# Where the last four outputs of an attention stage stand in the program order of the stage behind it

## What is computed

```python
x = L0_attn_x
x = _layernorm(x + _L0_attn_ref(x, ...), axis=-1)      # stage A: chunked linear attention
x = _layernorm(x + _L0_ffn_ref(x, ...), axis=-1)       # stage B: fp8 feed-forward
x = _layernorm(x + _L1_attn_ref(x, ...), axis=-1)      # stage C: causal softmax attention, one head of 128
x = _layernorm(x + _L1_ffn_ref(x, ...), axis=-1)       # stage D: base matrix + shared and routed low-rank parts
```

## Time and profile before

| | us |
|---|---|
| median of 3 runs | 1538.15 (1537.54 to 1539.66) |
| the profiled execution's own time | 1542.17 |
| its span, first to last instruction | 1540.5 |
| PE busy | 1470.2 (95%) |
| DVE busy | 1007.8 (65%) |
| ACT busy | 734.6 (48%) |
| POOL busy | 342.3 (22%) |
| mean granted TensorE clock | 0.984 |

### The profile page before, as it was taken

One profiled execution on the slowest core, in us unless ns is written; L12 is line 12 of the kernel. 1 busy time (PEld: TensorE's weight loads), 2 busy tenths in 40 slices (PEclk: granted clock), 3 DMA queues, 4 the chain that ended last, 5 costly groups with the idle time before them and its releaser, 6 DMA issues.

```text
span 1540.5 us, 23863 instructions
## 1 busy us (share of the span) xinstructions
PE 1470.2 (95%) x9484; PEld 1008.8 (65%) x9484; DVE 1007.8 (65%) x1967; ACT 734.6 (48%) x1040; POOL 342.3 (22%) x259
## 2 busy tenths in 40 slices
PE   8999999999999978899999999999999999999998
PEld 6677777777777766444555554546666665667886
DVE  3355646464645354897787778774888888666665
ACT  4333333332333323688768867863433444432333
POOL 0021212121111122000000000000666776760001
PEclk9999999999999999999999999999999999999999
DMA  7203031213030250101001101002300000000112
GB/s 266 80 27 108 27 108 55 83 52 107 29 107 13 75 191 13 37 0 56 28 29 55 55 1 55 1 26 74 91 1 1 1 1 1 0 1 28 55 55 82
DMA packets 43904, 79.93 MB, mean 52 GB/s; under 512 B 7073, under 2 KB 14881, under 8 KB 42386
## 3 DMA queue, kind: packets, MB, share of 16 engines
q1 hardware_dynamic: 43794, 78.41, 14.9%
HBM read 53.24 MB, written 25.17 MB: 51 GB/s over the span
## 4 chain that ended last, share of the span: by engine, by line
PE 61%; issue 19%; DVE 14%; ACT 3%; POOL 2%; DMA 0%; SPq 0%; DVEq 0%; POOLq 0%; ACTq 0%
PE psum L125 12%; PE psum L127 12%; PE psum L126 12%; PE psum L1335 6%; PE psum L978 3%; PE psum L985 3%; DVE sm L447 3%; PE psum L594 2%; PE psum L1313 2%; PE psum L620 2%; PE psum L615 2%; PE psum L609 2%; DVE c_mx L1256 1%; PE psum L624 1%; PE psum L629 1%
## 5 line engine op out<-in xcount | busy, mean ns | idle before, releaser
L978 PE MATMUL psum<-early,high 128*128 128x512 fp8e4 x1024 | 234.9, 382 | 10.2 <-DVE low_r L950 4.1
L978 PEld LDWEIGHTS psum<-early,high 128*128 128x128 fp8e4 x1024 | 98.2, 98 | 132.4 <-ACT early L857 6.6
L1184 POOL TENSOR_TENSOR c_ls<-c_ls,c_pr 128x512 f32<-128x512 f32 (+2 forms) x136 | 161.8, 1190 | 63.9 <-ACT c_pr L1229 54.5
L393 POOL TENSOR_TENSOR rms<-ms,mhalf 128x16 f32<-128x16 f32 x32 | 93.1, 2910 | 365.6 <-DVE ms L456 365.6
L1229 ACT ACTIVATE c_pr<-c_sc 128x512 f32<-128x512 f32 (+2 forms) x144 | 85.1, 594 | 151.5 <-DVE c_sc L1271 136.5
L1335 PE MATMUL psum<-c_pr,V 128*128 128x512 f32 (+2 forms) x288 | 138.3, 566 | 3.7 <-ACT c_pr L1229 2.5
L125 PE MATMUL psum<-Qh_r,Kh 128*128 128x512 f32 (+1 forms) x272 | 140.0, 515 | 0.0
L1271 DVE TENSOR_TENSOR c_sc<-psum,c_mb 128x512 f32<-128x512 f32 (+2 forms) x144 | 91.8, 640 | 42.8 <-PE psum L127 32.8
L985 PE MATMUL psum<-high,b_act 128*128 128x512 fp8e4 x512 | 117.3, 383 | 2.4 <-DVE Ql_r L955 2.2
L125 PE MATMUL psum<-early_r,high_r 128*128 128x512 f32 x256 | 107.1, 418 | 5.5 <-DVE early_r L419 5.5
L126 PE MATMUL psum<-Ql_r,Kh 128*128 128x512 f32 (+1 forms) x272 | 104.9, 386 | 0.0
(11 more groups left out here) (230 smaller groups left out, 3250.7 us busy)
## 6 DMA issues: line engine op xcount, KB each, us to landing
low<-x_dram SPq DMA_DIRECT2D x9, 1024.0 KB, 5.6
wst<-in_L_ffn_w_gating SPq DMA_DIRECT2D x16, 512.0 KB, 4.6
xs<-in_L_attn_x SPq DMA_DIRECT2D x8, 1024.0 KB, 7.9
xt<-in_x_turned SPq DMA_DIRECT2D x7, 1024.0 KB, 4.8
x_dram<-xs SPq DMA_DIRECT2D x7, 1024.0 KB, 4.8
x_dram<-low SPq DMA_DIRECT2D x5, 1024.0 KB, 4.3
wst<-in_L_ffn_w_linear SPq DMA_DIRECT2D x16, 256.0 KB, 4.6
high<-x_dram SPq DMA_DIRECT2D x4, 1024.0 KB, 6.4
```

The source lines that it names most:

```text
L393: nc.gpsimd.tensor_tensor(rms[:, :], ms[:, :], const["mhalf"][:, 0:H], ALU.pow).then_inc(*done)
L978: last = t.matmul(out[:, h, :], w8g[:, tile + k, (2 * m + h) * P:(2 * m + h + 1) * P], x8[:, u, k, :], start=k == 0, stop=k == DC - 1)
L1184: nc.gpsimd.tensor_tensor(ls[:, i % 2, q0:], ls[:, i % 2, q0:], pr[:, g % SLOTS, q0:], ALU.add).then_inc(*L.done(*name))
```

## The change

The plan's two lines that placed the four outputs of block 7, in pairs around hN, rb and rr of chunk 1 of block 0, are replaced by a loop that puts one output behind each of (rr, 0, 1), (rr, 0, 3), (rr, 1, 1) and (rr, 1, 3). The PSUM banks of the four outputs become 0, 5, 0, 5 in place of 7, 0, 1, 2.

```diff
         elif kind == "y" and i == NB - 1:
-            w = (7, 0, 1, 2)[name[2]]
+            w = (0, 5, 0, 5)[name[2]]
         else:
             w, n_m = (3, 4, 7)[n_m % 3], n_m + 1
...
         plan += part("D", ("hT", 0), ("rb", 0, 0)) + [("C", ("L", last))] + part("D", ("rb", 0, 0), ("h", 1))
-        plan += part("C", ("L", last), ("y", last, 1)) + part("D", ("h", 1), ("rr", 0, 1)) + part("C", ("y", last, 1), None)
-        plan += part("D", ("rr", 0, 1), None)
+        for c, (end, begin) in enumerate(zip([("rr", 0, 1), ("rr", 0, 3), ("rr", 1, 1), ("rr", 1, 3)], [("h", 1), ("rr", 0, 1), ("rr", 0, 3), ("rr", 1, 1)])):
+            plan += part("D", begin, end) + [("C", ("y", last, c))]
+        plan += part("D", ("rr", 1, 3), None)
```

## The result

The changed kernel takes 1542.98 us (median of 7 runs, 1542.18 to 1547.06), the kernel before 1537.85 (7 runs): +5.1 us, a ratio of 1.0034 with a 95% interval of 1.002 to 1.0047. The loss is small, but the whole interval lies above 1.

A forecast was written before the change was run, and what follows sets the result against it. After TensorE's last wait, a fixed run of matmuls sets the end. Later start of h of block 3 2.54, clock 1.7 and 2.4, sum +6.6 us; on the 1538.15 median that gives 1544.8, range 1540.5 to 1547.0.

The forecast's parts named there:

- Steps 1 to 5: TensorE from hN of block 1 to h of block 3: five new waits, the old one gone, h of block 3 +2.54.
- the walk: The new order followed job by job with prices from one execution; new waits 8.8 us, h of block 3 starting at 1432.74.
- The tail: Behind attention's last output y3: statistics, power, nb, four normalisations, delaying hh and hl; 6.68 us from y to hl.
- the old wait: In the kernel before, TensorE's 3.2 us wait on DVE ahead of h of block 2, plus 2.5 of slow clock.
- Step 3: At h of block 2: xl ready at 1405.85, so the 3.2 wait and its 2.5 of slow clock go; nothing else late.
- The clock: Slow clock after new waits: 1.7 (0 to 1.7) for the wait of 2.0, 2.4 (0.9 to 3.4) at block 3.
- rival (a): Waits as walked, but the clock holds over the wait of 2.0: +4.9, 1543.1 us; chance 0.14.
- step 5: The same tail one block later: rr of block 2 waits 3.35 for hl2, h of block 3 waits 1.8.
- Rival (b): Clock also costs nearly nothing around h of block 3: +2.5 to +3.0, 1540.7 to 1541.2 us; chance 0.09.
- (d): The order doesn't reach the engines, since a helper cuts each list by jobs: no difference, 1538.2 us; chance 0.03.
- step 2: At x of block 2: the fourth x needs bank 5 and waits 2.0 until DVE has read y1.
- Rival (c): Attention's tail is covered in its new place, at rr0 of block 2: -4.6, 1533.5, or -0.9; chance 0.12.

The follow-up runs named there:

- e3: Kernel before, with nb and the four normalisations of attention's block 7 moved behind rr of chunk 1 of block 1; 0.9962 of the kernel before, median 1533.1 us.
- e2: Changed kernel, with nb and the four normalisations of attention's block 7 one block later, behind rr of chunk 1 of block 2; 0.9997 of the kernel before.
- e1: Changed kernel with the four outputs in banks 0, 7, 0, 3 in place of 0, 5, 0, 5; 1.0046 of the kernel before.
- e4: Changed kernel with banks 0, 7, 0, 3 and also nb and the four normalisations behind rr of chunk 1 of block 2; 0.9994 of the kernel before.
- after_again: Changed kernel unedited, timed and profiled once more; 1.0035 of the kernel before, median 1544.77 us.
- e5: Changed kernel with only the four normalisations on ACT one block later, nb left behind var; 1.0001 of the kernel before.
- e6: Kernel before, with y3 and its tail alone moved behind rr of chunk 3 of block 1, in bank 5; 1.0019 of the kernel before.

## Why the prediction was right, and where it was off

**What bounds the kernel** held: past the last wait everything is a fixed amount of work. From the end of h of block 3 to the end of the span it is 1541.1 - 1433.57 = 107.5 us after; e3 and e2, with quite other waits, have the same (1534.7 - 1427.26 = 107.4 and 1537.4 - 1429.88 = 107.5).

**Steps 1 to 5.** All five waits are where the walk put them, and the four normalisations start at 1421.89, which is 1426.15 in the times of the kernel before; 1426 to 1428 was said. For the waits the walk said 0.85, 2.0, 0.8, 3.35 and 1.8; the profile has 0.69, 1.85, 0.51, 3.18 and 1.13. The first four are short by 0.15 to 0.3: the profile counts idle time from the end of the last record, the walk from the next possible issue, and a record is 0.16 longer than that (0.39 against 0.23); the remaining 0.13 at the read of y3 I leave open. The fifth is short by 0.7 because rr of block 2 ran on the fallen clock: it took 1.35 us to the end of its last record, in place of 0.87 at the full clock (1429.50 to 1430.37 in the kernel before), and so filled part of the wait for xl, which ends when DVE ends. So the start of h of block 3, the sum of the walk, is the better test: +2.54 said, 57.87 - 55.25 = +2.62 from the mark measured.

**The tail** as the cause of the last two waits was shown by e2_tail_late, and the same cause for the old wait by e3_pairs_tail_late. Step 3, that nothing else is late at h of block 2, is right, but only by 0.5 us: with the bank's wait of 1.85 gone, the xl behind DVE's queue make h wait 1.36 (e1, e4).

**The clock** is the term that was mis-sized. For the wait of 2.0 the sum had 1.7 in full. In the four profiles that have that wait it fell in three (after_again, e2, e5) and held in the first; the timed median, 5.1 against 6.6 forecast, says that it often held there or was partly absorbed, but timed runs have no trace, so how often stays open. The measured +5.1 is nearer rival (a)'s 4.9 than the sum; this term was taken at the upper end of its bounds, 0 to 1.7, and in the first profile it was 0. The forecast of 1544.8 lies 1.8 above the median; 0.3 of that is the kernel before, whose median is 1537.85 with more runs in place of 1538.15. For step 5 the sum had 2.4, and h of block 3 lost 5.01 - 2.75 = 2.26. With 2.62 and 2.26 the first profile's +4.86 is accounted for in full; that is rival (a), which said 4.9. Rival (b) is out, since h of block 3 was slow in both profiles of the changed kernel (5.01 and 4.39 us), and so is (d), since every job stands where the walk had it. The 4.0 between the profiled execution and the median, which the forecast carried over, does lie ahead of the edit: the two profiles differ by 4.26 at the mark.

**The split of the loss.** y3 and its tail one block on are worth +1.9 (e6). The rest, 4.86 - 1.86 = 3.0 in the first profile, is a difference and not a run: it comes with the other three outputs, whose new waits are 0.69 (hN without cover for hn) and 1.85 (y1 on DVE ahead of the xl of block 2). No run moves one of these alone. The wait of 1.85 moves but doesn't go with other banks (e1, e4): 1.85 becomes 1.36. Thus the bank named in step 2 was right for where TensorE stood, and wrong if read as the whole cause: but for 0.5 us it is DVE's order.

**Rival (c)** didn't happen, but e2 and e4 show what it needed: the tail taken off the path by hand.

## What to carry to other kernels

The end of a stage that is merged into the next one is not its last matmul but its last step on each in-order engine: place the statistics' tail (here one power, one nb and four normalisations; from y to hl 6.7 us) where ACT and DVE have room, and not by the matmul it belongs to. When a wait vanishes under another order, walk the same chain in its new place before counting the gain; and when a semaphore names a PSUM bank, ask which engine's queue keeps the bank, since another bank may only hand the wait on.

## What the runs showed of the hardware

The same instructions don't see the same clock. Over the same wait of 1.85 us, in the same work, the granted clock stayed at 1.00 in one profile and was 0.83 over the 10 us in three others. Ahead of the mark, where all these programs are alike, their profiles differ by 4.6 us (mark at 1370.62 in e1_banks, at 1375.22 in e4_banks_tail). Part of that is the clock. Between 1020 and 1040 us the granted clock was 0.91 in the profile of the kernel before and 1.00 in that of the changed one, and over this stretch the lag of the first behind the second grew from 2.67 us (the same L985 matmuls at 1034.24 and 1031.57) to 4.36 (L1313 at 1046.71 and 1042.35):

```profile
1020.00:1040.00 20.00, 17.80 (x83) 0.91 0.18 54
```

```profile
1020.00:1040.00 20.00, 17.47 (x91) 1.00 0.28 78
```

The timed runs say the same of whole executions. Of the kernel before, those with a mean granted clock of 0.984 took 1541.8 to 1542.7 us, with 0.987 1539.2 to 1539.9, with 0.989 or 0.990 1536.6 to 1538.4.

So two single spans of this kernel, 1540.5 and 1541.1, say nothing of a change of 5 us; a mark ahead of the edit does. The Trainium skill ("TensorE: Matmul & The Clock Gate", "What's actually happening") calls the point of transition variable from run to run; the rows agree.
